# Loading the key stacks ahead of the query stacks for the second half of the heads

## The reference

```
q = split_heads(x1 @ Wq.T)            # 16 heads of 16
k = split_heads(ctx @ Wk.T); v = split_heads(ctx @ Wv.T)
scores = q @ k.T / sqrt(16)           # 512 x 1601 per head, masked
out = softmax(scores) @ v             # joined, then @ Wo.T
x2 = layernorm(x1 + out @ Wo.T)
x3 = layernorm(x2 + base(x2) + adapter(x2))   # adapter = argmin of eight losses
```

## Time and profile before

| | us |
|---|---|
| median of 3 runs | 1637.96 (1634.35 to 1639.19) |
| profiled execution, its own time | 1639.14 |
| span of the profiled execution | 1636.6 |
| PE busy | 1577.6 (96%) |
| DVE busy | 1287.8 (79%) |
| ACT busy | 1044.5 (64%) |

### The profile page before, as it was taken

The page is one execution under the profiler, slowest core; times in us unless marked ns, Lnnn a source line. Parts: engine busy times, 40 slices in busy tenths (PEclk is TensorE's granted clock), DMA queues, the critical chain, the costliest instruction groups (busy, mean ns, idle before and its releaser), DMA issues.

```text
span 1636.6 us, 25498 instructions
## 1 busy us (share of the span) xinstructions
PE 1577.6 (96%) x9560; PEld 582.7 (36%) x9560; DVE 1287.8 (79%) x1905; ACT 1044.5 (64%) x1984; POOL 162.5 (10%) x153
## 2 busy tenths in 40 slices
PE   6778999999999999999999999999999999999997
PEld 5442323332333333332334323432333323332234
DVE  5788887888789878888788877888778877887523
ACT  2226777766666676776666666666666676666661
POOL 6311000100011000100001000100001000000000
PEclk9889999999999999999999999999999999999999
DMA  5556162543417171452607152261707234160010
GB/s 157 114 137 107 60 96 54 94 108 55 98 28 140 48 119 33 84 131 36 113 16 140 63 89 64 65 115 49 128 11 117 57 55 84 50 79 5 10 33 16
DMA packets 118664, 125.21 MB, mean 77 GB/s; under 512 B 35187, under 2 KB 100340, under 8 KB 118541
## 3 DMA queue, kind: packets, MB, share of 16 engines
q1 hardware_dynamic: 117724, 123.06, 38.1%
q10 hardware_dynamic: 816, 0.53, 0.1%
HBM read 84.18 MB, written 35.03 MB: 73 GB/s over the span
## 4 chain that ended last, share of the span: by engine, by line
PE 88%; DVE 5%; ACT 4%; DMA 2%; issue 1%; POOL 1%; SPq 0%; POOLq 0%; DVEq 0%
PE banks L1129 24%; PE values L1148 24%; PE banks L1089 12%; PE work L1019 5%; PE work L1005 5%; PE work L964 4%; PE work L1026 3%; ACT xprobs L1267 3%; PE work L1032 3%; DVE xneg_max_pieces L1452 2%; PE work L1011 2%; PE work L1035 1%; DMA max_dram<-xneg_max_rows 1%; PE work L1044 1%; PE work L949 1%
## 5 line engine op out<-in xcount | busy, mean ns | idle before, releaser
L1267 ACT ACTIVATE xprobs<-banks 128x512 f32<-128x512 f32 x1664 | 900.6, 595 | 407.9 <-PE banks L1129 403.9
L1452 DVE TENSOR_REDUCE xneg_max_pieces<-banks 128x2 f32<-128x1024 f32 x768 | 908.5, 1218 | 209.4 <-PE banks L1089 205.6
L1129 PE MATMUL banks<-xq_stacks,xk_stacks 99*128 99x512 bf16 (+1 forms) x1664 | 518.4, 385 | 11.4 <-ACT xprobs L1267 3.5
L1148 PE MATMUL values<-xprobs,xv_rows 128*17 128x512 f32 x3328 | 437.9, 598 | 1.6 <-ACT xprobs L1267 1.6
L1129 PEld LDWEIGHTS banks<-xq_stacks,xk_stacks 99*128 99x128 bf16 (+1 forms) x1664 | 127.3, 97 | 394.9 <-ACT xprobs L1267 285.7
L1089 PE MATMUL banks<-xk_stacks,xq_stacks 49*128 49x512 bf16 (+1 forms) x2048 | 251.3, 335 | 13.9 <-DVE xneg_max_pieces L1452 11.6
L1089 PEld LDWEIGHTS banks<-xk_stacks,xq_stacks 49*128 49x128 bf16 x2048 | 57.5, 94 | 344.7 <-DVE xneg_max_pieces L1452 226.2
L1148 PEld LDWEIGHTS values<-xprobs,xv_rows 128*17 128x17 f32 x3328 | 55.1, 95 | 124.4 <-issue 118.8
L1523 POOL TENSOR_TENSOR xk_parts<-xk_rest,xk_parts 128x401 bf16<-128x401 f32 (+1 forms) x64 | 59.1, 923 | 376.3 <-ACT xk_parts L1246 376.3
L1518 POOL TENSOR_TENSOR xrstd<-xrstd,mhalf 128x4 f32<-128x4 f32 x21 | 21.2, 1012 | 594.4 <-DVE xrstd L1321 594.4
L1019 PE MATMUL work<-xvT,ctxT_a 128*128 128x128 f32 (+1 forms) x416 | 56.8, 281 | 2.0 <-DVE xk_rest L1399 1.9
(11 more groups left out here) (299 smaller groups left out, 1040.7 us busy)
## 6 DMA issues: line engine op xcount, KB each, us to landing
xk_stacks<-key_parts_dram SPq DMA_DIRECT2D x186, 200.1 KB, 10.3
key_parts_dram<-xk_parts SPq DMA_DIRECT2D x144, 100.0 KB, 2.1
xq_stacks<-parts_dram SPq DMA_DIRECT2D x186, 64.0 KB, 5.9
ctxT_a<-in_ctxT SPq DMA_DIRECT2D x4, 1601.0 KB, 7.7
ctxT_b<-in_ctxT SPq DMA_DIRECT2D x4, 1601.0 KB, 8.0
parts_dram<-xq_parts SPq DMA_DIRECT2D x45, 128.0 KB, 1.8
key_parts_dram<-xk_parts SPq DMA_DIRECT2D x48, 100.2 KB, 9.5
xa<-in_x SPq DMA_DIRECT2D x8, 512.0 KB, 8.9
```

The lines of the kernel that those rows point to most:

```text
L1129: pe.matmul(at, kst[0:ROWS[par], k, h2, par, t * P:(t + 1) * P], qst[0:ROWS[par], k, h2, par, :], start=True, stop=True).then_inc(made, 1)
L1148: last = pe.matmul(av[32 * j:32 * j + HD + 1, :], vals[:, k, t, gr * GH + j, :], probs[:, sl % 2, j, :], start=t == 0, stop=t == XKT - 1)
L1267: nc.scalar.activation(probs[:, sl % 2, j, :], score_bank(n)[0], ACT.Exp).then_inc(exped, 1)
L1452: nc.vector.tensor_reduce(nmp[:, of % 2, :, j2, q, piece], pairs[n % MRING][:, :, :], AX.X, ALU.max, negate=True).then_inc(on["mxr"], 1)
```

## The change

It concerns only `sp_stacks`, and in it only c = 1 with b from 1 to 7: the last branch's order (query top, inverses, key top, query low, key low) is replaced by the order that c = 0 has (key top with mask rows, query top, inverses, query low, key low). The wait for the query parts is moved behind the key top rows.

```
             if b:
                 sp_key_parts_out(2 * (b - 1) + 1 + c)
-                if c:
-                    nc.sync.wait_ge(on["qparts_out"], 48 * (2 * (b - 1) + 1 + c))
             if b or c:
                 before = GROUPS * b - (NG if c == 0 else 0)
                 if before:
                     nc.sync.wait_ge(made, GH * XKT * before)
-            if b and not c:
+            if b:
                 sp_key_stacks(b, c, True)
                 nc.sync.wait_ge(on["qparts_out"], 48 * (2 * (b - 1) + 1 + c))
                 sp_query_stacks(c, True)
                 if between is not None:
                     sp_spread_inverses(between)
                 sp_query_stacks(c, False)
                 sp_key_stacks(b, c, False)
                 return
```

## The result

The changed kernel takes 1678.53 us, the median of 3 runs (1672.15 to 1681.79), against 1637.96 us. The ratio is 1.0241, with a 95% interval from 1.0213 to 1.0269. It is slower, as forecast, but by 40.6 us and not by 13.7, and outside the range.

A forecast was written before the change was run, and what follows sets the result against it. The prediction took PE, busy for 96% of the span, to bound the kernel. Stalls of 14.6 us less 0.9 coming back gave +13.7 us on the median 1637.96: 1651.7, forecast as 1651.5, range 1641 to 1663.

The forecast's parts named there:

- What would show it: Signs in seven second-half loads: late L1657, DVE idle 1.4 to 2.4 us before L1345, PE idle equally long before L964.
- S: The prediction's time zero: the start of SP's first stack load, 1239.25 for b = 6 in the kernel before.
- the 7 to 9: SP's timeline, b = 1 to 7: 7 to 9 us forecast between L1653 (inverses' write) and L1657 (the spread).
- The issue of the spread: SP's L1657, second-half loads: queue drained at S + 13.9, spread issued at S + 15.1 to 16.1, taken as S + 15.6.
- the term for the spread's own landing: From L1657's issue to its rows being there for DVE's L1345: 2.75 us, bounds 2.3 to 3.3.
- third rival: Second-half loads: slower queue or spread sharing engines, stalls of 3 to 4 us, 1660 to 1669 us; PE's clock included; chance 0.10.
- My 14.6 us of stall: DVE at L1345, PE behind it: 9.25 us over five batches, 2.2 at b = 6, 3.2 at b = 7.
- the wait for the maxima at b = 6: PE's 0.89 us wait for the maxima's rows at the second group's start, forecast to vanish, giving back 0.9 us.
- The page that spoke for no change: Key top rows at 341 GB/s: 7 us, spread issued near S + 13.5, there at S + 16.3; no cost in six batches.

## Why the prediction was right in kind and wrong in size

**The chain of causes was right.** SP stands longer for the write of the sums, the spread is issued late, DVE waits, PE waits behind it. The places named in "What would show it" are the right ones: L1657 at S + 15.1 to 16.1 in six batches of seven (12.99 in one, for which I have no reason) against a forecast of 15.6; idle time at L1345 put down to `err<-rsum_dram`, longer than forecast in six of the seven; PE's idle time before L964. Two sizes there were not: SP stood 5.65 and 6.60 us at b = 6 and 5, below the 7 to 9, and a batch grew by up to 8.3 us, not by 2. Moving the inverses to the front removed it to within 0.27%, moving them behind the keys in the old order brought it back (1.021 against 1.0241, intervals that overlap); this is shown, not argued.

**The issue of the spread came out right partly by luck.** The sum had 1.97 us for the x1 rows. But the same sum without them gives S + 13.1 to 14.1 for the first-half loads, and these take 14.7 in the mean before the change and 14.8 after it; the second-half loads of the changed kernel take 15.2. By this comparison the x1 rows added 0.4 us and the rest of the sum was about 1 us short, and the two errors nearly cancelled. No run leaves the x1 rows out, so their share is not shown.

**The step that failed first is the term for the spread's own landing.** I put 2.75 us from issue to landing, and bounds of 2.3 to 3.3. It is 5.0 in the mean. Three things were wrong. The one spread that I read the earlier trace rows was among the two fastest of its kind: the kernel before has eleven with nothing behind them, and their packets end 2.78 to 3.53 us after the issue, 3.22 in the mean. I took the last byte for the signal; with the low rows held back DVE starts 0.46 us after the last byte, 3.66 after the issue. And the sum had nothing for what stands behind the spread; the bounds had at most 0.96 us for it. Query rows behind it bring 5.0, key rows 5.8 to 7.1. The trace of the kernel before could have told me: in its seven first-half loads with query rows behind, the spread's packets end after 3.80 us in the mean. The term is short by 2.2 us in each of seven batches, 16 us. My 14.6 us of stall should have been about 30; 28.8 were measured.

**The second is the clock.** I listed it under the third rival with no price. 12.0 us were lost in the slots after the stall. In them the granted clock was at the lower level for a time, in all batches but b = 6, which lost nothing; and with PE kept at work the loss fell to 5.4 us, 4.6 of it in the three batches where the clock fell again. The whole 40.6 us are these two terms, 28.8 and 12.0, within 2 us. Both belong to my third rival (chance 0.10), whose stalls of 3 to 4 us were about right, and whose upper end of 1669 left the clock out.

**What came back.** I took off 0.9 us for the wait for the maxima at b = 6. That place is gone with L1627 at S + 32.49. The profile of the changed kernel has a wait of 1.65 us of that kind at 254.77, behind a first-half load, but S at b = 1 is not later for it (302.29 against 302.38). The term was right, and too small to matter.

**The page that spoke for no change.** The Trainium skill, page "DMA: Bandwidth & Descriptors", section "Bandwidth", gives 6.15 us for 1 MB, measured on transfers that GpSimd issued. The prediction's 7 us for the keys are an estimate from this figure. Put into the prediction's own sum in place of 10.3 they give an issue at an estimated S + 11.8 to 12.8, not near S + 13.5 as it says. The trace does not agree with it: the measured issue, S + 15.2 in the mean, is near the 15.6 that the trace's own 136 GB/s gave. The same page, section "Anatomy of one DMA — SWDGE (gpsimd) path", says for transfers issued by GpSimd that the signal comes only when the last byte is confirmed, and puts the fixed cost mostly there. On SP's queue the traces agree in kind: 0.46 us from the last byte to DVE with nothing behind, and 1.9 with key rows behind. This is one of the things that my term left out.

## What to carry to other kernels

When a transfer is moved in a queue, look for the small one behind it that an engine waits for, and write down its deadline: the order of two large loads was worth nothing here, the place of 8 KB and 128 KB among them 40 us. Measure a landing at the consumer that waits for it, not at the last packet, expect it to come later when large transfers are issued right behind, and do not take a single case for it. And a stall of TensorE costs more than its length when it lowers the clock: here 28.8 us of waiting became 41.

## What the runs showed of the hardware that I had not expected

- The same 128 KB transfer, always first in an empty queue, reached its consumer after 3.40 to 4.05 us with nothing issued behind it, 4.59 to 5.67 us with six 64.0 KB query loads behind it, and 5.76 to 7.07 us with 200.1 KB key loads behind it. Its first packet came after 1.35 to 1.42 us in all of these; the delay is in its later packets and behind the last one. With nothing beside it four packets of 4 B come with it and the DMA share is 0.25, so it seems to use four engines of 16; that these are then shared with what comes behind would explain the delay, but no run shows it.
- TensorE's clock fell to the lower level after idle times of 2.04 and 1.88 us (four key loads ahead, b = 6 and 3) and stayed at 1.00 through one of 2.14 us (low rows held back, b = 5) and one of 1.53 (four key loads ahead, b = 4). The same length can go either way.
- Ten matmuls of 0.23 us each, whose results nobody reads, placed ahead of a wait, made the changed kernel faster, from 1.0241 to 1.0171 of the kernel before, measured in two sessions. The size is loose: 11 us by the ratios, 6 us by the times, and "after it" fell by 6.6 us.
